# Issuing all row scatters of a routing unit one behind the other

## What is computed

```python
x = x + _L0_xattn_ref(_layernorm(x), ctx, ctx, Wq, bq, Wk, bk, Wv, bv)
x = x + _L0_ffn_ref(_layernorm(x), W_router, b_router, experts_inter, experts_out)
# inside _L0_ffn_ref, T = 8192 tokens, e = 8 experts, capacity = 1280:
top_vals, top_idx = jax.lax.top_k(softmax(logits), 2)
order = jnp.argsort(-routing_mask, axis=0, stable=True)
sorted_idx = order[:capacity]
inputs_tokens = x_flat[used_tokens] * mask_flat[:, None]
hmid = jax.nn.relu(jnp.einsum('ceh,ehi->cei', inputs_tokens, experts_inter))
out = jnp.einsum('cei,eih->ceh', hmid, experts_out) * inputs_weights[:, :, None]
combined = jnp.zeros((T, h)).at[used_tokens].add(out.reshape(-1, h))
```

## Time and profile before

| | us |
|---|---|
| median of 3 runs | 413.33 |
| lowest, highest | 410.4, 415.86 |
| the profiled execution, its own time | 408.41 |
| its span, from the first to the last instruction | 406.7 |
| GpSimd busy | 221.0 |
| TensorE busy | 289.4 |
| VectorE busy | 225.9 |
| ScalarE busy | 211.4 |

### The profile page before, as it was taken

One profiled execution on the slowest core, in us unless ns is written; L12 is line 12 of the kernel. 1 busy time (PEld: TensorE's weight loads), 2 busy tenths in 40 slices (PEclk: granted clock), 3 DMA queues, 4 the chain that ended last, 5 costly groups with the idle time before them and its releaser, 6 DMA issues. The chain is left out here.

```text
span 406.7 us, 6739 instructions
## 1 busy us (share of the span) xinstructions
PE 289.4 (71%) x2205; PEld 242.7 (60%) x2205; DVE 225.9 (56%) x892; ACT 211.4 (52%) x431; POOL 221.0 (54%) x197
## 2 busy tenths in 40 slices
PE   1679889897979797771005999999999896971000
PEld 0456566675756565551004999999999896970000
DVE  3477997979797979666002655555555452530000
ACT  3367858585858575622002676767676554650000
POOL 3000266354636666556640383868668686858681
PEclk9989888898989898856556999999999996997555
DMA  5103744243434442211006356374664542423341
GB/s 178 62 2 103 204 120 131 91 130 112 134 106 121 126 130 67 80 50 30 10 0 188 108 72 145 34 157 78 114 146 38 101 39 26 39 28 33 27 38 13
DMA packets 50707, 34.68 MB, mean 85 GB/s; under 512 B 4701, under 2 KB 46298, under 8 KB 50672
## 3 DMA queue, kind: packets, MB, share of 16 engines
q1 hardware_dynamic: 35120, 22.75, 19.7%
q0 software_dynamic: 14592, 11.16, 18.7%
q10 hardware_dynamic: 960, 0.33, 0.3%
HBM read 18.82 MB, written 16.58 MB: 87 GB/s over the span
## 5 line engine op out<-in xcount | busy, mean ns | idle before, releaser
L393 POOL DMA_INDIRECT out_dram<-y_sb,token x80 | 123.4, 1543 | 64.0 <-issue 37.4
L353 POOL DMA_INDIRECT slots_dram<-rows,place_no x96 | 94.1, 980 | 112.7 <-DVE place_no L693 50.0
L779 DVE SCALAR_TENSOR_TENSOR hid_lo<-ps,hid_hi 128x1024 fp32r<-128x1024 f32 x40 | 49.0, 1224 | 57.0 <-ACT hid_hi L483 57.0
L483 ACT ACTIVATE hid_hi<-ps 128x1024 fp32r<-128x1024 f32 x40 | 41.2, 1029 | 36.7 <-PE ps L910 36.7
L859 PE MATMUL ps<-wkv_sb,ct_sb 128*128 128x256 f32 x128 | 53.1, 516 | 6.4 <-DMA ct_sb<-ctx_t_dram 5.4
L908 PE MATMUL ps<-xgt_hi,wi_hi 128*128 128x256 f32 x160 | 49.2, 308 | 0.0
L929 PE MATMUL ps<-hid_hi,wo_hi 128*128 128x256 f32 x160 | 49.0, 306 | 0.0
L909 PE MATMUL ps<-xgt_lo,wi_hi 128*128 128x256 f32 x160 | 46.0, 287 | 0.0
L910 PE MATMUL ps<-xgt_hi,wi_lo 128*128 128x256 f32 x160 | 45.8, 286 | 0.0
L930 PE MATMUL ps<-hid_lo,wo_hi 128*128 128x256 f32 x160 | 45.4, 284 | 0.0
L931 PE MATMUL ps<-hid_hi,wo_lo 128*128 128x256 f32 x160 | 45.4, 283 | 0.0
(11 more groups left out here) (118 smaller groups left out, 641.5 us busy)
## 6 DMA issues: line engine op xcount, KB each, us to landing
xg<-slots_dram SPq DMA_DIRECT2D x8, 576.0 KB, 4.7
ct_sb<-ctx_t_dram SPq DMA_DIRECT2D x16, 256.0 KB, 3.8
out_dram<-rows SPq DMA_DIRECT2D x16, 256.0 KB, 2.9
x_sb<-x_dram SPq DMA_DIRECT2D x15, 256.0 KB, 4.0
wi_sb<-w_in_dram SPq DMA_DIRECT2D x8, 256.0 KB, 4.9
wo_sb<-w_out_dram SPq DMA_DIRECT2D x8, 256.0 KB, 5.2
slots_dram<-rows,place_no POOLq DMA_INDIRECT x96, 2.3
out_dram<-y_sb,token POOLq DMA_INDIRECT x80, 3.3
```

The costliest lines, as they stand in the source:

```text
L353: pool.indirect_dma_start(slots[:, :], bass.IndirectOffsetOnAxis(ap=place_no[:, u % PLACES_RING, j:j + 1], axis=0), rows[:, c % ROWS_RING, ...
L393: pool.indirect_dma_start(out[:, :], bass.IndirectOffsetOnAxis(ap=token[:, e, j:j + 1], axis=0), y_sb[:, e % 2, j, :], None, compute_op=AL ...
L483: act.activation(hid_hi[:, i % 2, :], [ps0, ps1][i % 2][:, :], ACT.Relu).then_inc(hid_high, 1)
L779: dve.scalar_tensor_tensor(hid_lo[:, i % 2, :], [ps0, ps1][i % 2][:, :], 0.0, hid_hi[:, i % 2, :].bitcast(F32), ALU.max, ALU.subtract).the ...
```

## The change

The count by quarters goes. Each unit has one semaphore, `rows_sent[u]`, which reaches 16 times the number of the unit's scatters when all have landed. `scatter(u)` issues its 8 or 16 indirect DMAs with no wait between them. All other waits stay where they were and ask for the unit's full count in place of its last quarter's. No instruction is added, and none changes its place: 32 semaphores become nine, and ahead of GpSimd's scatters 23 waits between quarters are taken out of the program, of which 17 are passed in this run, since units 7 and 8 are left out.

```diff
-def quarters(u):
-    return UNITS[u][1] * G * TOP_K // QUARTER
+def scatters(u):
+    return UNITS[u][1] * G * TOP_K
...
-        rows_sent = [[sem(f"rows_sent{u}_{q}") for q in range(quarters(u))] for u in range(LAST + 1)]
+        rows_sent = [sem(f"rows_sent{u}") for u in range(LAST + 1)]
...
-                for j in range(number * G * TOP_K):
-                    c, q = first + j // (G * TOP_K), j // QUARTER
-                    if j % QUARTER == 0 and q > 0:
-                        pool.wait_ge(rows_sent[u][q - 1], 16 * QUARTER)
+                for j in range(scatters(u)):
+                    c = first + j // (G * TOP_K)
                     pool.indirect_dma_start(
...
-                    ).then_inc(rows_sent[u][q], 16)
+                    ).then_inc(rows_sent[u], 16)
...
-                        pool.wait_ge(rows_sent[u][-1], 16 * QUARTER)
+                        pool.wait_ge(rows_sent[u], 16 * scatters(u))
...
-                    dve.wait_ge(rows_sent[unit_of(a - ROWS_RING)][-1], 16 * QUARTER)
+                    w = unit_of(a - ROWS_RING)
+                    dve.wait_ge(rows_sent[w], 16 * scatters(w))
...
-                        dve.wait_ge(rows_sent[p2 - PLACES_RING][-1], 16 * QUARTER)
+                        dve.wait_ge(rows_sent[p2 - PLACES_RING], 16 * scatters(p2 - PLACES_RING))
```

More of the change, by code:

```diff
@@ L42 @@
 PG = PAIR * P
-QUARTER = 4
 STEPS = range(-1, CHUNKS + 3)
@@ L370, in _ @@
                         if not may_be_full(w):
-                            pool.wait_ge(rows_sent[w][-1], 16 * QUARTER)
+                            pool.wait_ge(rows_sent[w], 16 * scatters(w))
                     pool.wait_ge(last_counted, 1)
```

## The result

The prediction said 388 us, faster. The changed kernel took **459.8 us** (median of 4 runs, 458.2 to 462.1), against 414.6 for the kernel before beside it (410.4 to 417.7, 4 runs): a ratio of 1.113, 95% interval 1.102 to 1.124. It is 11% slower. The profiled execution took 459.24 us (span 457.5), that is 50.8 more than that of before, 408.41. Further down, the ranges of the kernel before leave out three executions of a slower state (415.9, 417.0 and 418.0 us).

The account below looks back on a forecast made before the run. The prediction took GpSimd, delayed by waits for its own scatters, to bound the kernel. An earlier L896 (24.75 us) plus 0.5 us gave 25.3 us, hence 388 us from the 413.33 median; range 381 to 398.

Parts of the forecast that it names:

- GpSimd's pace: Front half: scatters without waits every 1.274 us, units starting 0.78 us behind hand-over, last scatter at 179.6 instead of 210.16.
- rivals B and D: GpSimd's scatters: B, pace stretches, 393 us, chance 0.10; D, transfers' queue keeps mean pace at 1.665 us, 413 us, chance 0.04.
- The transition: Between the halves: load of `xg` issued at 185.1 to 187.7, L896 at 191.4 instead of 216.15, 24.75 us earlier.
- The clock: TensorE's clock, half at the expert half's start, counted nothing; its rival, lower clock in the expert half: 408 us, chance 0.03.
- The front half itself: Other engines in the front half: denser scatters do not slow VectorE, landing waits only get easier; counted as nothing.
- rival E: Front half: GpSimd's denser issue slows VectorE; a quarter longer gives 424 us, slower than before; chance 0.02.
- my sum for the profiled execution: Whole kernel: 24.75 + 0.5 = 25.3 us gained from 408.41, giving 383.1 us.
- Case A: Whole kernel as summed, steady scatter pace and no queue building up: 388 us, range 383 to 392, chance 0.81.

Follow-up runs that it names:

- the two runs on one chip: On chip 13: changed kernel with waits ahead of every fourth scatter, 411.5 us; kernel before without waits between quarters, its quarter semaphores kept, 456.6 us.
- unit-semaphore run: Changed kernel, one semaphore per unit, but GpSimd again waits for all landings so far ahead of every fourth scatter of a unit; 411.5 us.
- marker run with signal: Changed kernel with a small memset behind each scatter that raises a semaphore for which nobody waits; 382.5 us.
- two-queued: Changed kernel with a signalling memset behind each scatter; scatter j waits for the memset behind scatter j-2; 374.6 us on one chip, 462.6 on another.
- marker run: Changed kernel with a one-column memset behind each scatter, with neither wait nor signal; 467.3 us.
- quarters of eight: Kernel before with eight scatters between waits in place of four, nothing else changed; 434.5 us.
- four open: Changed kernel, but scatter j waits until scatter j-4 of its unit has landed, nothing else between scatters; 460.5 us.
- at most two open: Changed kernel, but scatter j waits until scatter j-2 of its unit has landed, no memset; 405.7 us on one chip, 409.1 on another.

## Why the prediction was wrong

**GpSimd's pace, right.** 1.273 us a scatter, 0.77 us behind the hand-over, and no slower for running without a pause (966 to 1158 ns). So rivals B and D fall. The rule of the Trainium skill that was weighed there (page "DMA: Bandwidth & Descriptors", section "SWDGE vs HWDGE vs iDMA", VectorE holding GpSimd's descriptor writes up) changes nothing here either: the median scatter takes 967 or 968 ns in all three traces of the kernel after, and the longest took 1158, 1327 and 1425, against 1247 in the trace of before.

**The transition, right.** The load of `xg` is issued 6.1 us ahead of its first use, and the 24.86 us wait is gone.

**The clock, right in kind.** The expert half is at 1.00 up to 350 us and at 0.90 over its whole length, as before, and 168.2 us long from 281.13 to 449.3 (before: 168.8).

**"The front half itself", wrong, and this is the step that failed.** I priced what the denser stream does to the other engines at nothing, and rival E at 0.02, on the ground that VectorE's L571 keeps its 676 to 689 ns. It kept them in the kernel after as well. I had asked only whether an operation gets longer, not whether its start comes later. The cost was no operation of VectorE but the wait for a signal, 13.3 us in each unit (33.7 against 20.4). The sum of E, 424 us, had the right sign and place (the distance of the hand-overs, named there as what would show it), the wrong mechanism, and half the size: the front half grew by 267.2 - 191.1 = 76.1 us, and not by a quarter (36); by the two runs on one chip it is 53.2.

**Was there something to see beforehand?** The trace of before has five runs of eight without a pause, and no late signal beside any. The unit-semaphore run has eights of the same kind with late signals beside them. I took the first for evidence that a dense stream does no harm, from one trace that, by its complete record of landings, was most likely of the undisturbed kind; on chip 15 the kernel before shows none either. A stream of eight undisturbed on one chip is no evidence for another.

**On chips of the other kind the chain of the working holds.** The marker run with signal, at 382.5 us, stands beside my sum for the profiled execution, 383.1. That the totals agree so well is in part luck: the kernel before took 404.4 us beside it and not 408.4, so the gain is 21.9 us where I forecast 25.3, and the two-queued kernel gained 30.5 (374.6 against 405.1). The timelines of GpSimd, SyncE and TensorE:

```profile
179.82 0.97 POOL L352 DMA_INDIRECT slots_dram<-rows,place_no  x1 [0.19 <-issue]
...
185.49 0.37 SPq L285 DMA_DIRECT2D xg<-slots_dram  x1
...
190.88 1.09 PE L897 MATMUL ps<-ident,xg 128*128 128x128 f32 x4
...
204.35 1.58 POOL L393 DMA_INDIRECT out_dram<-y_sb,token  x1 [23.45 <-ACT y_sb L493]
```

Forecast were 179.6, 185.1 to 187.7, 191.4 and 204.5. Case A thus describes two of seven chips, as far as the nearest kernel shows, and what it leaves out on the other five, some 53 to 76 us in the front half, is two to three times what it gains.

**No version beat both kernels everywhere.** The best on the undisturbed kind (two-queued, 374.6 against 405.1) is among the slowest on the late kind (462.6). Of those run on the late kind none was faster than the kernel before by more than 1%; the pauses between quarters, which look like pure loss in the trace, are what limits the loss in the front half there.

## What to carry to other kernels

Before taking out a wait that looks useless, ask what its pause gives the other engines, and look in the trace for later starts and for waits with an unnamed releaser, not only for longer operations. Compare kernels only where they ran on the same chip: here one program differed by 88 us between two chips, more than any two kernels on one of them. A queue of indirect DMAs from GpSimd should be timed on several chips, with and without pauses between groups of four. And look whether a trace names its landings: here one without them was of the late kind in every case that could be told.

## What the runs showed of the hardware

- On five of seven chips, a stream of GpSimd's indirect scatters (128 rows of 576 bytes each, 1.27 us apart) without pauses makes TensorE's signals to ScalarE and VectorE late, from about the fourth or fifth scatter until about the last has landed (read in the kernel after and the two-queued one). The longest wait for one was 10.6 to 13.1 us in three traces of the kernel after, and 15.9 in the marker run. The hand-overs come every 33.7 to 35.2 us then, where 20.4 is undisturbed. VectorE's signals to itself and to ScalarE are on time in the three traces of the kernel after, but come up to 1.9 us late in the unit-semaphore run and 2.7 with quarters of eight. The scatters' landings are less than 5.1 us behind: with four open the stream kept its 1.27 us, and so the landing four back had come in time.
- At 1.41 us from scatter to scatter about three quarters of the delay are left (hand-overs every 30.7 us; 440.8 us against 462.3, on two chips). Mostly in fours with pauses of 1.9 us or more it is 3.4 us a unit (hand-overs every 23.9; 411.5 us), and with at most two open 1.6 (22.0; 409.1 us); the kernel before took 411 and 412 beside them.
- On two of seven chips such streams delay nothing, up to 72 scatters in a row at 1.27 us, and the kernel before itself is some 2% faster on them (402.4 to 405.1 against 409.2 to 416.7). No trace of the kernel before from a chip known to be of the late kind was taken, so whether the 2% come from late signals is open; its 408.4 us in a trace that looks undisturbed speaks against a sharp line between the two.
- The traces from the late kind hold only 3680 to 4160 updates of semaphores, against 5551 to 5675 on the other, and name no landing of a scatter.
- The scatter-adds of the expert half, at 1.84 us in tens, came with no late signals in any trace.
- Small memsets on GpSimd behind a scatter fit into its 0.30 us gap: one costs nothing, four make it 1.35 us, six 1.41.
